# A hybrid of deformable convolution, additive attention and routed experts on one core: shorter square roots, queries through a mask, four banks for the first image's front, and the last image's end as ranked steps

## The chip, the cores and the metric

The kernel runs on one core of a Trainium2 chip, in single precision. The metric is the device time of one execution, in microseconds (us). The kernel before takes 15566.36 us, the median of three runs (15549.57 to 15602.39).

The names of the engines in what follows: PE is TensorE (matrix products; PEld are its weight loads), DVE is VectorE, ACT is ScalarE, POOL is GpSimd, SP is SyncE, which issues most of the DMAs. A suffix q, as in DVEq, is an engine's sequencer, which handles waits and drains.

## What is computed

Eight images of 56 x 56 pixels and 128 channels, so 3136 tokens an image, go through two layers:

```
# layer 0
xp = x @ w_in + b_in
h  = gelu(batchnorm(depthwise3x3(x) + dw_b))
offset, mask = h @ w_off + b_off, softmax(h @ w_msk + b_msk)      # 4 groups x 9 samples
y  = sum over 9 samples of mask * bilinear(pad(xp), place + offset)
x  = x + gamma1 * layer_norm(y @ w_out + b_out)
x  = x + gamma2 * layer_norm(gelu(x @ w_fc1 + b_fc1) @ w_fc2 + b_fc2)
# layer 1, on t = tokens of x
u = ln(t); f = u @ W1[:128]; g = u @ W1[128:]                     # 16 columns each
e[i,j] = exp(tanh(f_i + g_j + b1) @ w2 + b2)  for j < i, else 0
t = t + (e / sum_j e) @ u
z = ln(t); p = softmax(z @ gate_w, over tokens)                   # 64 experts
each expert takes its top 8 tokens, pools them by p, runs 128-512-128 with gelu,
and adds p * result to those 8 tokens of t
```

Every layer norm and the batch norm need a reciprocal square root of a variance plus an epsilon. The attention's f is called the query, its g the key.

## The kernel before

**Tiling.** An image has 7 bands of 8 rows (`image_in`, `project_in`, the nine taps of `conv`, `offsets`, `weights`), 27 tiles of patches, 49 sample tiles of 64 positions and 25 blocks of 128 tokens (the last has 64). A band of x is transposed on TensorE (L1643, four transposes into one PSUM bank) and copied out by VectorE (L1199), projected (L1657, copied at L1207), and a patch tile is four transposes again (L1643), a copy by VectorE (L1215) and a DMA to DRAM (L949). From there GpSimd gathers the four corners of each sample by indirect DMA (L1104), 18 of them for a sample tile; VectorE multiplies them by their weights (L1285, six instructions) and adds them up (L1288). A block then goes through the chain of steps `turn`, `mix`, `turn_mid`, `hidden`, `mlp_out`, `turn_norm`, `keys`, which alternate between TensorE and VectorE in one PSUM bank (`chain_ps`). Attention takes keys and queries in units of one tanh on ScalarE (L1584) over 128 partitions, which are 8 rows of tokens by the 16 hidden values; TensorE multiplies by w2 (L1746), ScalarE takes exp (L1594), and TensorE turns it (L1643) and adds up the values (L1775); `finish` on VectorE ends the block.

**The root.** `rsqrt` (L1154 to L1165) is a bit trick and three Newton steps on one column: a sum (`var`, L1156), a scaled sum (`newton`, L1157), the first guess from the bits of `var` (L1159), and three times an instruction with two per-partition pointer operands (L1162) and one with one (L1164), with a `settle` (a drain, L1123) between them. A block calls it four times; with the one of the batch norm there are 801 calls.

**The queries.** `keys` on TensorE is one product with w_key (L1728, 128 columns) and eight with `w_query` (L1731, 16 columns each), which holds w_q in the columns of one of eight rows and zeros in the others: each of the eight picks every eighth token, so that the sum over the eight in PSUM has row q's query in partitions 16q to 16q+15. VectorE copies the keys (L1330) and adds b1 to the queries (L1331).

**The side bank.** All steps of SIDE (bands, patches, conv, offsets, routing, experts, combine) share one PSUM bank, `side_ps`: TensorE waits for its last reader (`side_free`) before each.

**The order.** Each engine executes its steps in an order that a planner works out when the kernel is built: `due_times` gives each step a time by which it is wanted, `needs` what it waits for, `LASTS` how long it is supposed to last, and `simulate` runs a list scheduling over several images, from which a period of two images is cut. Image 0 has an order of its own, images 1 to 6 are a loop of three double periods, and image 7 has the last order, into which `late_steps` put the routing of images 0 to 6 (u_), their experts (w_in, e_) and the combine (c_in, c_x, c_mix L1855, c_store; 49 combine steps, each one TensorE step of 4 instructions). What image 7 itself still needs after its last block is written by hand behind that: SP L1064 to L1081, VectorE L1489 to L1545, ScalarE L1607 to L1615, TensorE L1858 to L1925. In this order it is: max (L1491), exp on ScalarE (L1609) beside match_replace (L1495) and not_equal (L1497), the product (L1502), turns and pooling (L1643, L1867), then 16 steps of four experts each (L1805, L1811), whose weights arrive in five slots of which 11 are loaded again (L1051, L1054), the last mix (L1921) and the saves (L1080).

## Time and profile before

| | us |
|---|---|
| median of three runs | 15566.36 |
| the profiled execution | 15422.14 |
| its span, first to last instruction | 15420.3 |
| TensorE busy (matmuls) | 8049.2 (52%) |
| ScalarE busy | 6799.7 (44%) |
| GpSimd busy | 6705.1 (43%) |
| VectorE busy | 6160.4 (40%) |
| mean granted TensorE clock | 0.694 of full |

The busy times are sums over all instructions of an engine, in one execution. No engine is busy for much more than half of the span, so the sums alone don't say what sets the time; for that the profile follows the chain of waits back from the last instruction, and its shares are of the span. Times of single instructions come from the timeline, whose origin is the first instruction.

### The profile page before, as it was taken

How to read it: one execution, taken by the hardware profiler on the slowest of the kernel's cores; microseconds unless marked ns; L12 is line 12 of the kernel's file. 1: busy time of each engine (PE TensorE's matmuls, PEld its weight loads, DVE VectorE, ACT ScalarE, POOL GpSimd, SP SyncE). 2: the span in 40 equal slices, each digit the busy share in tenths (PEclk: the TensorE clock that was granted, in tenths of full speed). 3: DMA queues.
4: the chain of work that ended last, by engine and by line, in shares of the span. 5: the costliest groups of instructions: out<-in, count | busy, mean ns of one | idle time of the engine just before them, and what ended most of it. 6: DMA issues, size and time to landing. Idle time of an engine off the chain costs nothing.

```text
span 15420.3 us, 158696 instructions
## 1 busy us (share of the span) xinstructions
PE 8049.2 (52%) x48713; PEld 4360.0 (28%) x48713; DVE 6160.4 (40%) x17991; ACT 6799.7 (44%) x8233; POOL 6705.1 (43%) x7060
## 2 busy tenths in 40 slices
PE   3445554555644556445554555544555455544568
PEld 1222222222322223222232222222222222222234
DVE  3443334433344334433344433443434433444342
ACT  0234553445534555245443455434543345533454
POOL 4444344444444444444444444444444444444420
PEclk7566776667766777667676676667766667766778
DMA  1111111111111111111111111111111111211234
GB/s 57 41 50 35 31 40 41 48 34 33 40 42 47 34 34 42 44 42 32 37 42 46 40 34 37 42 46 38 32 40 40 49 35 31 57 54 53 76 105 144
DMA packets 453515, 711.92 MB, mean 46 GB/s; under 512 B 146641, under 2 KB 260754, under 8 KB 451026
## 3 DMA queue, kind: packets, MB, share of 16 engines
q0 software_dynamic: 225792, 462.87, 11.4%
q1 hardware_dynamic: 226866, 238.69, 4.9%
q8 instruction: 407, 6.67, 0.2%
q14 instruction: 450, 3.69, 0.1%
HBM read 595.03 MB, written 105.96 MB: 45 GB/s over the span
## 4 chain that ended last, share of the span: by engine, by line
another core or an unknown queue 35%; PE 18%; DVE 15%; ACT 13%; issue 13%; DVEq 5%; DMA 1%; SPq 0%; POOL 0%; ACTq 0%; POOLq 0%
ACT tanh L1584 12%; PE score_ps L1746 6%; DVEq L1123 5%; DVE pool_mem L1285 3%; DVE newton L1162 2%; PE value_ps L1775 2%; PE chain_ps L1731 2%; DVE rstd L1164 2%; PE turn_ps L1643 1%; PE chain_ps L1711 1%; PE side_ps L1674 1%; DVE bst L1169 1%; PE side_ps L1643 1%; PE chain_ps L1719 1%
## 5 line engine op out<-in xcount | busy, mean ns | idle before, releaser
L1584 ACT ACTIVATE tanh<-key_rep,query 128x896 f32<-128x896 f32 (+7 forms) x6400 | 5563.3, 951 | 5580.4 <-remote 2489.4
L1104 POOL DMA_INDIRECT pool_mem<-patches_even,pool_mem x3528 | 3352.2, 950 | 4120.9 <-DVE y L1288 2961.6
L1104 POOL DMA_INDIRECT pool_mem<-patches_odd,pool_mem x3528 | 3352.7, 950 | 4102.6 <-DVE y L1288 3079.5
L1746 PE MATMUL score_ps<-tanh,score_w 128*32 128x512 f32 (+3 forms) x24320 | 3530.2, 634 | 2116.0 <-ACT tanh L1584 1289.8
L1746 PEld LDWEIGHTS score_ps<-tanh,score_w 128*32 128x32 f32 x24320 | 819.4, 124 | 4196.5 <-issue 2606.8
L1285 DVE TENSOR_TENSOR pool_mem<-pool_mem 128x384 f32<-128x384 f32 x2352 | 1136.1, 553 | 41.2 <-issue 37.8
L1775 PE MATMUL value_ps<-values,expoT 128*128 128x129 f32 (+1 forms) x5200 | 1002.7, 342 | 258.7 <-issue 185.3
L1288 DVE TENSOR_REDUCE y<-pool_mem 128x64 f32<-128x2304 f32 x392 | 1000.9, 2553 | 38.3 <-issue 8.9
L1775 PEld LDWEIGHTS value_ps<-values,expoT 128*128 128x128 f32 (+1 forms) x5200 | 882.3, 244 | 355.5 <-issue 289.5
L1643 PE MATMUL turn_ps<-ident,expo 128*128 128x128 f32 (+1 forms) x2632 | 590.4, 348 | 727.5 <-ACT expo L1594 320.8
L1594 ACT ACTIVATE expo<-score_ps,tiny 128x896 f32<-128x896 f32 (+9 forms) x416 | 383.4, 922 | 1054.3 <-remote 713.4
L1352 DVE COPY expoT<-turn_ps 128x512 f32<-128x512 f32 (+4 forms) x800 | 456.3, 571 | 857.2 <-remote 568.6
L1162 DVE TENSOR_SCALAR newton<-rstd,newton 128x1 f32<-128x1 f32 (+1 forms) x2403 | 655.1, 273 | 231.9 <-issue 50.0
L1643 PEld LDWEIGHTS turn_ps<-ident,expo 128*128 128x128 f32 (+1 forms) x2632 | 396.1, 181 | 923.2 <-issue 361.1
L1330 DVE COPY key_rep<-chain_ps 128x128 f32<-128x128 f32 (+1 forms) x200 | 57.6, 288 | 1490.1 <-remote 1178.0
L1731 PEld LDWEIGHTS chain_ps<-chainT,w_query 128*128 128x128 f32 x3200 | 635.8, 303 | 0.0
L1731 PE MATMUL chain_ps<-chainT,w_query 128*128 128x16 f32 (+1 forms) x3200 | 620.6, 342 | 0.0
L1164 DVE TENSOR_SCALAR rstd<-newton,rstd 128x1 f32<-128x1 f32 (+1 forms) x2403 | 513.4, 214 | 230.5 <-issue 51.1
L1728 PE MATMUL chain_ps<-chainT,w_key 128*128 128x128 f32 (+1 forms) x400 | 137.7, 443 | 782.9 <-DVE chainT L1323 655.9
L1169 DVE BATCH_NORM_STATS2 bst<-chain_ps 128x6 f32<-128x128 f32 (+1 forms) x400 | 118.5, 296 | 1062.2 <-remote 677.1
L1594 ACT ACT_TABLE_LOAD x207 | 265.6, 1283 | 617.9 <-remote 451.6
L1323 DVE COPY chainT<-chain_ps 128x128 f32<-128x128 f32 (+1 forms) x200 | 57.1, 286 | 1176.2 <-remote 1075.5
(167 smaller groups left out, 7470.3 us busy)
## 6 DMA issues: line engine op xcount, KB each, us to landing
pool_mem<-in_weight SPq DMA_DIRECT2D x64, 1024.0 KB, 10.1
pool_mem<-patches_even,pool_mem POOLq DMA_INDIRECT x3528
pool_mem<-patches_odd,pool_mem POOLq DMA_INDIRECT x3528
patches_even<-pool_mem SPq DMA_DIRECT2D x104, 256.0 KB
patches_odd<-pool_mem SPq DMA_DIRECT2D x104, 256.0 KB
pool_mem<-in_x SPq DMA_DIRECT2D x56, 224.0 KB
x_tok<-in_x SPq DMA_DIRECT2D x192, 64.0 KB
x_d<-x SPq DMA_DIRECT2D x192, 64.0 KB
```

The lines of the kernel that those rows point to most:

```text
L1104: pool.indirect_dma_start(gathered[:, b, j * 4 * CG:(j + 1) * 4 * CG], None, patches_flat[int(odd)], bass.IndirectOffsetOnAxis(ap=index[:, ...
L1123: return v.drain()
L1162: v.tensor_scalar(newton[:r, 1:2], rstd[:r], rstd[:r], newton[:r, 0:1], ALU.mult, ALU.mult)
L1164: v.tensor_scalar(rstd[:r], newton[:r, 1:2], 1.5, rstd[:r], ALU.add, ALU.mult)
L1285: v.tensor_tensor(part, part, weight[:, lo:lo + PIECE].unsqueeze(2) .to_broadcast([P, PIECE, CG, 4]), ALU.mult)
L1288: v.tensor_reduce(y[:, i // 2 % 2, b].rearrange("p (g c) -> p g c", c=CG), product.rearrange("p (g t) c k -> p g c t k", g=2), AX_XY, ALU. ...
L1584: nc.scalar.activation(tanh[:, ui % TANH_SLOTS, :w], key_rep[:, lo:lo + w], ACT.Tanh, bias=query[:, col:col + 1]).then_inc(tanh_done.sem, 1)
L1594: nc.scalar.activation(expo[:r, ci % 2, :w], score_ps[:r, ci % 2, :w], ACT.Exp, bias=tiny[:r, 2:3])\
L1643: return mm(out, src, ident[:r, :r], is_transpose=True, start=True, stop=True)
L1731: last = mm(chain_ps[:, P:P + r // ROWS8], w_query[:, q].rearrange("p a b -> p (a b)"), chainT[:, q:r:ROWS8], start=q == 0, stop=q == ROWS ...
L1746: last = mm(score_ps[32 * col:32 * col + 32, ci % 2, lo:hi], score_w[:, place], tanh[:, ui % TANH_SLOTS, lo:hi], start=place == 0, stop=pl ...
L1775: last = mm(value_ps[:r, :C + 1], expoT[:wj, pi % 2, z, :r], values[:wj, value_place(odd, j)], start=j == 0, stop=j == k)
```

## The change

- **Roots.** `var` goes: the first guess is taken from the bits of `newton`'s first column with another constant. The first instruction of a Newton step becomes a scalar_tensor_tensor, with one pointer operand and one tensor of one column, the second a scalar_tensor_tensor with a constant and one tensor.
- **Queries.** One product with a w_q that is laid out eight times (128 columns), instead of eight of 16 columns. VectorE adds b1 and multiplies the 128 x 128 result by a mask of zeros and ones (`own_row`, a new constant that comes by one more DMA), drains, and adds up groups of eight columns. The zeroing of `w_query` and its eight copies at the start go.
- **Image 0's front.** Its 7 bands and 27 patch tiles take turns in four banks (the quarters of `score_ps`) with a count of reads of their own, and the patches are copied to four buffers, with a semaphore each, in place of two.
- **Image 7's end.** The part written by hand becomes steps with rank 0 (`l_in` to `l_save`) of the last order, the combine of images 0 to 6 gets the lowest rank (due at 40), the expert weights have four slots in place of five (12 loads again), exp works in place and is started only when not_equal is done, and the experts' results and chosen rows lie on 128 partitions with two DMAs for the results and the second biases.
- **Costs.** The planner's costs of `keys`, `mix`, `mlp_out` and `finish` change with the first two parts, so that the order of every image is worked out anew.

```diff
-RSQRT_MAGIC = 1597463007.0
+RSQRT_MAGIC = 1597463007.0 - 2.0 ** 30 - 2.0 ** 22
...
-LATE_SLOTS = 5
-ROUTE_AT = (4.0, 7.0, 10.0, 14.0)
+LATE_SLOTS = 4
+SLOTS_AT = (19600, 15504, 11408, 7312)
+ROUTE_AT = (2.0, 5.0, 8.0, 11.0)
...
+EARLY_BANKS = 4
...
-    ("pe", "turn_norm"): .35, ("pe", "keys"): 2.3, ("pe", "route"): .35, ("pe", "logits"): .45,
+    ("pe", "turn_norm"): .35, ("pe", "keys"): .9, ("pe", "route"): .35, ("pe", "logits"): .45,
...
+    ("dve", "l_max"): 10.5, ("act", "l_exp"): 3.3, ("dve", "l_mul"): 3.8, ("pe", "l_turn"): .9, ("dve", "l_turn"): .5,
...
-            able = [x for x in ready[e] if side_free or e != "pe" or x[2][0] not in SIDE]
+            able = [x for x in ready[e] if e != "pe" or x[2][0] not in SIDE or
+                    (banks[began % EARLY_BANKS] if x[1:] in early else side_free)]
...
     done = sum(len(images) for images in units)
+    when = 40.0
     for n in range(done):
-        when += COMBINE_GAP
+        when += .1
...
-        put(when + s * .01, "sp", ("w2_in", s), at("dve", "sample", NSUB - 1),
-            *([at("sp", "c_store", done - 1, q) for q in range(turns)] if s >= 3 else []))
+        put(25.0 + s * .01, "sp", ("w2_in", s), at("dve", "sample", NSUB - 1),
+            *([at("sp", "e_store", STEPS - 1)] if s >= 3 else []))
...
+    put(0, "sp", ("l_in",), *last_block)
+    put(0, "dve", ("l_max",), at("sp", "l_in"), at("dve", "u_last", last))
+    put(0, "act", ("l_exp",), at("dve", "l_max"))
+    put(0, "dve", ("l_mul",), at("act", "l_exp"))
...
+    for s in range(STEPS):
+        if s >= LATE_SLOTS:
+            put(s * .01, "sp", ("l_w", s), at("sp", "w2_in", LATE_SLOTS - 1), at("pe", "l_out", s - LATE_SLOTS))
...
...
-            v.memset(w_query[:], 0.0)
...
-            for i in range(ROWS8):
-                v.tensor_copy(w_query[:, i, i], w_q[:])
-
...
-                v.tensor_scalar(var[:r], src, EPS, None, ALU.add)
                 v.tensor_scalar(newton[:r, 0:1], src, EPS, -0.5, ALU.add, ALU.mult)
                 settle()
-                v.tensor_scalar(rstd[:r].bitcast(I32), var[:r].bitcast(I32), -0.5, RSQRT_MAGIC, ALU.mult, ALU.add)
+                v.tensor_scalar(rstd[:r].bitcast(I32), newton[:r, 0:1].bitcast(I32), -0.5, RSQRT_MAGIC, ALU.mult, ALU.add)
                 settle()
                 for _ in range(3):
-                    v.tensor_scalar(newton[:r, 1:2], rstd[:r], rstd[:r], newton[:r, 0:1], ALU.mult, ALU.mult)
-                    settle()
-                    v.tensor_scalar(rstd[:r], newton[:r, 1:2], 1.5, rstd[:r], ALU.add, ALU.mult)
+                    v.scalar_tensor_tensor(newton[:r, 1:2], rstd[:r], rstd[:r], newton[:r, 0:1], ALU.mult, ALU.mult)
+                    settle()
+                    v.scalar_tensor_tensor(rstd[:r], newton[:r, 1:2], 1.5, rstd[:r], ALU.add, ALU.mult)
                     settle()
...
                     v.tensor_copy(key_rep[:, at:at + r], chain_ps[:, :r])
-                    v.tensor_scalar(query[:, i * A:i * A + r // ROWS8], chain_ps[:, P:P + r // ROWS8], tiny[:, 0:1],
-                                    None, ALU.add)
+                    v.scalar_tensor_tensor(spread[:, :r], chain_ps[:, P:P + r], tiny[:, 0:1], own_row[:, :r], ALU.add, ALU.mult)
+                    settle()
+                    v.tensor_reduce(query[:, i * A:i * A + r // ROWS8], spread[:, :r].rearrange("p (g q) -> p g q", q=ROWS8),
+                                    AX_X, ALU.add)
                     settle().then_inc(keys_copied.sem, 1)
...
+                elif what == "l_max":
+                    dve.wait_ge(last_in, 16)
+                    v.max(top[:E], score7)
+                    settle()
+                    v.tensor_scalar(neg[:E], top[:E, 0:1], -1.0, None, ALU.mult)
+                    v.match_replace(chosen7, top[:E], score7, LOW)
+                    settle()
+                    v.tensor_tensor(chosen7, score7, chosen7, ALU.not_equal)
+                    settle().then_inc(last_top, 1)
...
-            v.tensor_scalar(neg[:E], top[:E, 0:1], -1.0, None, ALU.mult)
-            settle().then_inc(last_top, 1)
-            v.match_replace(chosen7, top[:E], score7, LOW)
...
+                    nc.scalar.activation(score7, score7, ACT.Exp, bias=neg[:E], accum_out=total[:E, 0:1])
...
+            def bank_free(n, step):
+
+                if not is_early(n):
+                    side_free()
+                    return side_ps[:]
+                at = early_steps.index(step)
+                if at >= EARLY_BANKS:
+                    pe.wait_ge(early_read, early_reads.index(early_steps[at - EARLY_BANKS]) + 1)
+                return early_bank[at % EARLY_BANKS]
...
-                    for q in range(ROWS8):
-
-                        last = mm(chain_ps[:, P:P + r // ROWS8], w_query[:, q].rearrange("p a b -> p (a b)"),
-                                  chainT[:, q:r:ROWS8], start=q == 0, stop=q == ROWS8 - 1)
-                    last.then_inc(keys_done.sem, 1)
+                    mm(chain_ps[:, P:P + r], w_q[:].rearrange("p a b -> p (a b)"), chainT[:, :r], start=True, stop=True)\
+                        .then_inc(keys_done.sem, 1)
...
+        "own_row": (np.arange(P)[:, None] // A == np.arange(P)[None, :] % ROWS8).astype(np.float32),
```

**Places where the order changes.** The first is the start of TensorE's program, image 0's bands and patches; `side_ps` and `score_ps` are PSUM, `pool_mem` and `early` hold the x bands, the padded planes and the depthwise taps. Rows with `ident` are transposes, 128x448 once is a projection, and 128x448 x9 is the depthwise conv. Before:

```order
L1643 MATMUL side_ps<-ident,pool_mem 128x112 x8
L1657 MATMUL side_ps<-pool_mem,early 128x448
L1643 MATMUL side_ps<-ident,pool_mem 128x112 x8
L1657 MATMUL side_ps<-pool_mem,early 128x448
L1643 MATMUL side_ps<-ident,pool_mem 128x112 x12
L1657 MATMUL side_ps<-pool_mem,early 128x448 x5
L1643 MATMUL side_ps<-ident,pool_mem 128x128 x104
L1643 MATMUL side_ps<-ident,pool_mem 36x128 x4
L1674 MATMUL side_ps<-pool_mem,early 128x448 x9
```

After:

```order
L1746 MATMUL score_ps<-ident,pool_mem 128x112 x8
L1760 MATMUL score_ps<-pool_mem,early 128x448
L1746 MATMUL score_ps<-ident,pool_mem 128x112 x8
L1760 MATMUL score_ps<-pool_mem,early 128x448
L1746 MATMUL score_ps<-ident,pool_mem 128x112 x8
L1760 MATMUL score_ps<-pool_mem,early 128x448
L1746 MATMUL score_ps<-ident,pool_mem 128x112 x4
L1760 MATMUL score_ps<-pool_mem,early 128x448 x4
L1746 MATMUL score_ps<-ident,pool_mem 128x128 x52
L1777 MATMUL side_ps<-pool_mem,early 128x448 x9
L1746 MATMUL score_ps<-ident,pool_mem 128x128 x52
L1746 MATMUL score_ps<-ident,pool_mem 36x128 x4
```

All of these steps go through `score_ps` now, transposes run further ahead of projections, and the first band's conv stands in the middle of the patches.

The second is the first `keys` step on VectorE, in image 0, with its neighbours (`key_rep` takes the keys, `query` the queries, `spread` is the masked product). Before:

```order
L1248 SCALAR_TENSOR_TENSOR pool_mem<-pool_mem,base_index 128x126
L1330 COPY key_rep<-chain_ps 128x128
L1331 TENSOR_SCALAR query<-chain_ps,tiny 128x16
L1285 TENSOR_TENSOR pool_mem<-pool_mem 128x384 x6
L1288 TENSOR_REDUCE y<-pool_mem 128x64
```

After:

```order
L1335 SCALAR_TENSOR_TENSOR pool_mem<-pool_mem,base_index 128x126
L1417 COPY key_rep<-chain_ps 128x128
L1418 SCALAR_TENSOR_TENSOR spread<-chain_ps,tiny,own_row 128x128
L1420 TENSOR_REDUCE query<-spread 128x16
L1280 COPY pool_mem<-side_ps 128x8x56
L1381 COPY chainT<-chain_ps 128x128
```

Two instructions stand where one did, and another patch copy and chain copy follow in place of a sample tile's products: the steps around it have moved too.

The third is the end of TensorE's program, from the last block's gate logits (L1787 before, L1887 after) on: the transposes and products of 64 columns are image 7's turns and pooling, and the rows of 112x128 are the combine (L1855 before, L1958 after). Before:

```order
L1787 MATMUL side_ps<-xln2T,gate_w 64x64
L1643 MATMUL score_ps<-ident,tanh 112x64 x8
L1867 MATMUL value_ps<-key_rep,tanh 64x128 x4
L1643 MATMUL score_ps<-ident,tanh 112x64 x4
L1867 MATMUL value_ps<-key_rep,tanh 64x128 x4
L1643 MATMUL score_ps<-ident,tanh 112x64 x4
L1867 MATMUL value_ps<-key_rep,tanh 64x128 x4
```

After, the same place, and then the end of the expert loop:

```order
L1887 MATMUL side_ps<-xln2T,gate_w 64x64
L1958 MATMUL side_ps<-pool_mem 112x128 x16
L1746 MATMUL score_ps<-ident,tanh 112x64 x8
L1978 MATMUL value_ps<-key_rep,tanh 64x128 x8
L1746 MATMUL score_ps<-ident,tanh 112x64 x8
L1978 MATMUL value_ps<-key_rep,tanh 64x128 x8
L1746 MATMUL score_ps<-ident,tanh 112x64 x8
L1978 MATMUL value_ps<-key_rep,tanh 64x128 x8
L1746 MATMUL score_ps<-ident,tanh 112x64 x4
L1958 MATMUL side_ps<-pool_mem 112x128 x4
L1978 MATMUL value_ps<-key_rep,tanh 64x128 x4
L1958 MATMUL side_ps<-pool_mem 112x128 x4
```

```order
L1913 MATMUL score_ps<-pool_mem,expoT 1x128 x16
L1746 MATMUL chain_ps<-ident,expo 128x128 x4
L1958 MATMUL side_ps<-pool_mem 112x128 x4
L1913 MATMUL score_ps<-pool_mem,expoT 1x128 x16
L1958 MATMUL side_ps<-pool_mem 112x128 x8
L2012 MATMUL score_ps<-x_tok,tanh 112x128 x28
L1958 MATMUL side_ps<-pool_mem 112x128 x4
```

Before, no combine step stands behind the last gate logits; now 13 of the 49 do: four ahead of the first turn, three among turns and pooling, two in the expert loop, and four around the last mix (L2012). Four more stand just ahead of the last logits, among the last block's turns of exp.

## Rows read from the trace of the kernel before

**Rows 1.** The page's busy times by engine.

```profile
PE 8049.2 (52%) x48713; PEld 4360.0 (28%) x48713; DVE 6160.4 (40%) x17991; ACT 6799.7 (44%) x8233; POOL 6705.1 (43%) x7060
```

**Rows 2.** The chain of waits, whole span: shares by line.

```profile
by line: another core or an unknown queue 35.3%; issue 12.7%; ACT tanh L1584 11.6%; PE score_ps L1746 6.3%; DVEq L1123 5.1%; DVE pool_mem L1285 2.7%; DVE newton L1162 2.5%; PE value_ps L1775 2.1%; PE chain_ps L1731 2.0%; DVE rstd L1164 1.9%
```

**Rows 3.** The page's groups: line, op, out<-in xcount | busy, mean ns | idle before.

```profile
L1104 POOL DMA_INDIRECT pool_mem<-patches_even,pool_mem x3528 | 3352.2, 950 | 4120.9 <-DVE y L1288 2961.6
...
L1162 DVE TENSOR_SCALAR newton<-rstd,newton 128x1 f32<-128x1 f32 (+1 forms) x2403 | 655.1, 273 | 231.9 <-issue 50.0
...
L1330 DVE COPY key_rep<-chain_ps 128x128 f32<-128x128 f32 (+1 forms) x200 | 57.6, 288 | 1490.1 <-remote 1178.0
...
L1731 PE MATMUL chain_ps<-chainT,w_query 128*128 128x16 f32 (+1 forms) x3200 | 620.6, 342 | 0.0
L1164 DVE TENSOR_SCALAR rstd<-newton,rstd 128x1 f32<-128x1 f32 (+1 forms) x2403 | 513.4, 214 | 230.5 <-issue 51.1
L1728 PE MATMUL chain_ps<-chainT,w_key 128*128 128x128 f32 (+1 forms) x400 | 137.7, 443 | 782.9 <-DVE chainT L1323 655.9
```

**Rows 4.** VectorE groups by form, same columns as rows 3.

```profile
L1187 DVE SCALAR_TENSOR_TENSOR ln_a<-chain_ps,mv,affine 128x128 f32<-128x128 f32 x384 | 134.8, 351 | 30.1 <-issue 1.3
...
L1331 DVE TENSOR_SCALAR query<-chain_ps,tiny 128x16 f32<-128x16 f32 x192 | 43.2, 225 | 0.0
...
L1228 DVE TENSOR_REDUCE pool_mem<-pool_mem 128x14 f32<-128x126 f32 x56 | 15.9, 284 | 6.6
...
L1178 DVE SCALAR_TENSOR_TENSOR early<-early,chan 128x1 f32<-128x1 f32 x1 | 0.2, 220 | 0.1
...
L1176 DVE TENSOR_TENSOR early<-rstd,chan 128x1 f32<-128x1 f32 x1 | 0.2, 160 | 0.1
```

**Rows 5.** Timeline of VectorE, one root: start us, us, engine, line, op.

```profile
5037.77 0.15 DVE L1156 TENSOR_SCALAR var<-mv 128x1 f32<-128x1 f32 x1
5037.84 0.14 DVE L1157 TENSOR_SCALAR newton<-mv 128x1 f32<-128x1 f32 x1
...
5038.30 0.27 DVE L1162 TENSOR_SCALAR newton<-rstd,newton 128x1 f32<-128x1 f32 x1
5038.65 0.21 DVE L1164 TENSOR_SCALAR rstd<-newton,rstd 128x1 f32<-128x1 f32 x1
5038.94 0.27 DVE L1162 TENSOR_SCALAR newton<-rstd,newton 128x1 f32<-128x1 f32 x1
```

**Rows 6.** Timeline of one keys step on TensorE.

```profile
4997.01 3.43 PE L1731 MATMUL chain_ps<-chainT,w_query 128*128 128x16 f32 x16
```

**Rows 7.** Timeline of all engines after that step.

```profile
5026.76 0.95 POOL L1104 DMA_INDIRECT pool_mem<-patches_even,pool_mem  x1 [0.30 <-issue]
5032.91 0.29 DVE L1330 COPY key_rep<-chain_ps 128x128 f32<-128x128 f32 x1 [32.45 <-remote]
```

**Rows 8.** Windows: stretch, its length, busy us of engines, clock, DMA share, GB/s.

```profile
0.00:51.60 51.60, 19.90 (x42) 8.16 (x43) 22.41 (x55) 0.00 (x0) 0.20 (x4) 1.00 0.24 66
51.60:104.70 53.10, 30.02 (x108) 19.05 (x108) 17.99 (x26) 0.00 (x0) 0.00 (x0) 1.00 0.33 127
...
15043.50:15260.00 216.50, 211.59 (x1298) 129.28 (x1300) 61.93 (x144) 173.24 (x177) 0.00 (x0) 0.91 0.42 122
```

**Rows 9.** Window of the last expert loop's transfers.

```profile
15324.00:15386.00 62.00, 40.86 (x524) 21.10 (x528) 13.63 (x35) 2.59 (x12) 0.00 (x0) 0.78 1.04 372
```

**Rows 10.** Timeline of image 0's patches.

```profile
55.49 1.12 PE L1643 MATMUL side_ps<-ident,pool_mem 128*128 128x128 f32 x4 [0.83 <-DVEq L1123]
56.65 0.69 DVE L1215 COPY pool_mem<-side_ps 128x512 f32<-128x512 f32 x1 [1.25 <-PE side_ps L1643]
```

**Rows 11.** Timeline of GpSimd: the first gather.

```profile
124.10 1.08 POOL L1104 DMA_INDIRECT pool_mem<-patches_even,pool_mem  x1 [123.64 <-DVEq L1123]
```

**Rows 12.** Groups by line: the combine on TensorE.

```profile
L1855 PE MATMUL side_ps<-pool_mem 64*112 64x128 f32 x392 | 93.0, 384 | 1.7 <-issue 1.0 <-DVEq L1123 0.7
```

**Rows 13.** Timeline of ScalarE: image 7's softmax.

```profile
15290.65 2.91 ACT L1609 ACTIVATE pool_mem<-tanh,early 64x3136 f32<-64x3136 f32 x1 [23.26 <-DVEq L1123]
```

More of the change, by code:

```diff
@@ L410, in simulate @@
     for n, engine, step in todo:
-        before = {(n - age, e, s) for age, e, s in need[engine, step]} & known
+        before = {(n - age, e, s) for age, e, s in need.get((n, engine, step), need[engine, step])} & known
         waiting[n, engine, step] = len(before)
@@ L725, in network @@
         bias1 = late.take(E * (HID // P)).rearrange("p (e c) -> p e c", e=E)
-        bias2 = late.take(C)[:E]
+        bias2 = late.take(C)
         acc = late.take(C)
```

419 lines of the change are left out of this document (243 added, 176 removed).

## The prediction

> **What bounds the kernel now.** I read the busy times first. TensorE is busy for 52% of the span, ScalarE 44%, GpSimd 43%, VectorE 40% [rows 1]: no engine sets the time alone, so a saving counts only where its engine is what the others wait for. The chain of waits says where: 35.3% of the span is waiting that no instruction explains, 11.6% the tanh, 6.3% its product with w2, 5.1% VectorE's drains; of what the change touches, L1162 has 2.5%, L1164 1.9% and the queries' product L1731 2.0% [rows 2]. The unexplained part has a pattern. At 4997.01 TensorE does the queries of a block and is done at 5000.44 [rows 6]; VectorE's copy that waits for them starts at 5032.91, 32.45 us idle, and the last gather of a burst started at 5026.76 [rows 7]. A gather takes 0.95 us and 0.30 until the next, so the 18 of a sample tile are a burst of 22.5 us, and 392 tiles are 8820 us, 57% of the span [rows 3, 7]. A hand-over from TensorE inside a burst can thus come late by more than any edit here saves, and what is gained ahead of it is then given back. Over the 200 blocks that copy idles 1490.1 us, 1178.0 of it released by nothing visible [rows 3].
>
> All sums are made against the profiled execution, 15422.14 us; the median of the runs is 15566.36, 0.93% above it, and I carry a difference in us over to the median unchanged.
>
> **Roots.** Of the first two instructions, which start 0.07 us apart, one goes [rows 5]: 0.07 us. The instruction with two pointer operands takes 273 ns, with one 214 [rows 3]. On one column, a scalar_tensor_tensor with one pointer and a tensor takes 220 ns, and a tensor_tensor without a pointer 160 [rows 4]. So each of three pairs becomes 380 from 487 ns, 0.107 less, and the gaps between them (the pair's starts are 0.35 and 0.29 apart, 0.08 above the durations [rows 5]) stay: 0.07 + 3 x 0.107 = 0.39 us a root, 801 roots, 312 us of VectorE. Its two lines hold 4.4% of the chain, 679 us, of 1168.5 busy [rows 2, 3]: 58% of them lie on the path. 0.58 x 312 = 181 us. The bounds are nothing (the forms cost the same as now) and 312.
>
> The Trainium skill, "ScalarE: Activation LUTs", section "What ACT_TABLE_LOAD costs", says that on ScalarE each per-partition pointer operand adds about 93 ns. The rows above show about 60 on VectorE, so the measured number goes into the sum; by 93 the roots would give about a half more.
>
> **Queries, TensorE.** 16 passes of 16 columns take 3.43 us at the lower clock of that stretch [rows 6]; over the span L1731 is busy 620.6 us for 200 blocks. The new product has the form of L1728, busy 137.7 for 200 [rows 3]. That is 483 us less. L1731's share of the chain is 2.0%, 308 us, half of its busy time [rows 2, 3], so 240 us on the path; bounds 0 and 483.
>
> **Queries, VectorE.** The addition of 16 columns, 225 ns, gives way to 128 columns from PSUM with a pointer and a tensor, 351 (L1187), a drain of about 0.1 (the gaps above), and a reduction as L1228's 126 columns, 284 [rows 4]: 0.51 us more, 102 us over 200 blocks. Every tanh of the block waits behind it, and so does the next block's `turn`, which needs chain_ps free; I take 60% as on the path, 60 us, bounds 40 and 102. The eight copies and the zeroing at the start are about 2 to 4 us, against one more constant to load: nothing.
>
> Steady part: -181 - 240 + 60 = -361 us if the chain's shares are taken at their word. But 57% of the time is burst, and there a step that is done earlier may only wait longer for the same hand-over. I count the part outside (43%) whole and the part inside by half: 0.715 x 361 = 258 us.
>
> **The new order of all images.** The planner's costs for four steps change and with them every period. No row prices that. The nearest is the unexplained wait itself, 35.3% or 5443 us: a tenth more or less of it would be 540 either way. I take 0, and keep it for the range.
>
> **Image 0's front.** The bands end at 51.60 and the patches at 104.70 [rows 8]: 53.1 us for 27 patches, 1.97 each. In one of them TensorE works 1.12 us and is idle 0.83 before it, for VectorE's copy of 0.69 and the drain behind it [rows 10]: the two take turns because there is one bank. With four, TensorE, the slower, goes on: 27 x 0.83 = 22 us less. The 7 bands are 14 steps with the same kind of copy between them: 14 x 0.83 = 12 us less. And the first conv stands between patches now, so that its gelu and offsets run beside them; before, 19.4 us lay between the end of the patches and the first gather at 124.10 [rows 8, 11]. Of that I take 6. Together 40 us. The share of the DMA queues there is 0.33 at 1.97 a tile [rows 8]; at 1.14 it would be 0.57, so they hold. If each patch still waits for its store, half is left: bounds 20 and 48. What follows waits for nothing else, so this is carried to the end.
>
> **Image 7's end.** From 15043.50 to 15260 TensorE is busy 211.59 of 216.50 us [rows 8]: there it is the bound, and the combine is on it. The combine's 49 steps are x392, busy 93.0, so 1.90 us each [rows 12]. In the new order 13 stand behind the last gate logits and 4 just ahead of them: 17 x 1.90 = 32 us out of that stretch. What takes them in: four lie in front of the first turn while VectorE works (free), two in the expert loop, which waits for DMA (free), three among turns and pooling and four around the last mix: 7 x 1.9 = 13 us, of which I take 10; the four among the last turns half, 4. Then exp of 2.91 us, which ran beside match_replace, comes behind not_equal: +3 [rows 13]. And the DMA queues, full for 62.0 us (share 1.04) with 11 loads [rows 9], get a twelfth: +5.6. -32 + 10 + 4 + 3 + 6 = -9; with what is freed earlier in the stretch by the shorter roots nothing, since TensorE bounds it. Bounds -35 and +20.
>
> **Sum.** -258 - 40 - 9 = -307: 15115 for a profiled execution, 15566 - 307 = 15,260 for the median.
>
> **Rivals.**
>
> A, the bursts swallow it: hand-overs inside bursts end with the burst whatever comes before, and of the part outside only half meets no other wait. 361 x 0.43 x 0.5 = 78, with 49 of the ends 127: 15,440. For it: the 32 us of [rows 7] against a saving of 3. Against it: the chain passes through L1162, L1164 and L1731 for 987 us, so they are often what is waited for.
>
> B, everything counts: VectorE and TensorE are in order, and whatever shortens the chain of one block lets the next sample tile's products, and so the next burst, start earlier. 312 + 483 - 102 = 693, with 49: 742, so 14,825. For it: GpSimd idles 4120.9 us on one parity's gathers, mostly for VectorE's products [rows 3].
>
> C, slower: the new order puts more hand-overs from TensorE behind bursts. Its place is the periods of images 1 to 6, its price the length of such a wait, up to 32 us [rows 7]. It decides from 307 us more, 5.6% of the 5443, or one such wait for every 20 blocks of the 200 (10 x 32). With 8% it is +435 - 307 = +128: 15,695. For it: no cost of the planner stands for a late hand-over, so its places are chance. Against it: the order before was made by the same rule, so the chance is even on both sides, and needs 5.6% to win.
>
> D, VectorE's new forms hold up the gathers. Each root has six instructions with two tensors from SBUF where it had none: 6 x 0.19 x 801 = 913 us, 57% of it in bursts, 520 us. A gather that falls on one (520 / 1.25 = 416 of them) would start later by half of its length, 0.1 us: 40 us, so 15,300; 10% of the weight. If each instruction held up a whole burst by its full length it were +520, and slower by 213.
> That a VectorE instruction with two SBUF inputs takes a port pair that GpSimd needs, and blocks it for its whole length, is in the Trainium skill, "SBUF — State Buffer", in the list on the diagram of the ports; rows 7 show gathers 1.25 us apart, but none beside such an instruction, so they don't settle it.
>
> **How the numbers follow.** The forecast has 0.46, A 0.22, B 0.10, C 0.12, D 0.10 (nearly all of it faster). About 0.3%, 47 us, is what a measurement of this kernel can tell from no change. Within it lies the upper end of A with an unlucky order: 0.07. Slower is C with 0.12 and 0.01 of D: 0.13. Faster is the rest, 0.80. The range starts between the forecast and B, 14,970, and ends at 15,560, which leaves most of C and half of B outside.
>
> **What would show it.** Roots: each VectorE pair 380 ns with gaps of 0.08, a root 2.06 us; wrong if the forms take 273 and 214 as before. Queries: two passes and busy about 140 us in place of 620; the wait of the keys' copy tells A (unchanged at about 7.5 us a block) from B. Front: the first gather near 84 in place of 124. End: 17 combine steps after the last keys' stretch, the expert loop's full queues some 68 us long. The order: the share of unexplained wait, 35.3%, up in C. Gathers further apart than 1.25 us would be D. The prediction is wrong if what lies between the first gather and the last stretch (124.10 to 15043.50 [rows 8, 11]) shortens by less than 80 or more than 600 us.

## The result, and the profile after

The changed kernel takes 15361.55 us, the median of four runs (15339.42 to 15399.26), against 15557.97 of the kernel before in its four: a ratio of 0.9879, 95% interval 0.9853 to 0.9904, 196 us less. The forecast was 307 us less. The sign and the order of size came out, but two of its large terms did not, and it will be seen that their errors took each other away in large part.

The two profiled executions stand oddly to this: 15422.14 us before, 136 below its median, and 15399.26 after, 38 above its own. Compared to each other they would give 23 us. So only the two ends are compared from trace to trace, and the middle is what is left of the difference of the medians. In the traces of related kernels below the start repeats within 3 us (121.92 to 124.10 with the old front, 72.12 and 74.45 with the new), the end less well.

The changed kernel's busy times from the page, and two of its groups (columns as in [rows 3]):

```profile
PE 7675.1 (50%) x45913; PEld 3859.4 (25%) x45913; DVE 5935.6 (39%) x17381; ACT 6773.1 (44%) x8210; POOL 6700.8 (44%) x7060
...
L1243 DVE SCALAR_TENSOR_TENSOR newton<-rstd,newton 128x1 f32<-128x1 f32 (+1 forms) x2403 | 528.3, 220 | 211.4 <-issue 34.9
...
L1245 DVE SCALAR_TENSOR_TENSOR rstd<-newton,rstd 128x1 f32<-128x1 f32 (+1 forms) x2403 | 385.7, 161 | 222.0 <-issue 31.8
```

Against [rows 1], TensorE has 374 us less and VectorE 225 less. The root's instructions take 220 and 161 ns where they took 273 and 214 [rows 3]. The timeline of one root on VectorE:

```profile
5012.25 0.15 DVE L1238 TENSOR_SCALAR newton<-mv 128x1 f32<-128x1 f32 x1
...
5012.71 0.22 DVE L1243 SCALAR_TENSOR_TENSOR newton<-rstd,newton 128x1 f32<-128x1 f32 x1
5013.01 0.16 DVE L1245 SCALAR_TENSOR_TENSOR rstd<-newton,rstd 128x1 f32<-128x1 f32 x1
5013.24 0.22 DVE L1243 SCALAR_TENSOR_TENSOR newton<-rstd,newton 128x1 f32<-128x1 f32 x1
```

A pair starts 0.53 us after the last (5012.71 to 5013.24), where it was 0.64 [rows 5]; the whole root, to the end of its last instruction at 5014.24, is 1.99 us. The groups of the `keys` step (TensorE, then VectorE):

```profile
L1832 PE MATMUL chain_ps<-chainT,w_q 128*128 128x128 f32 (+1 forms) x400 | 117.6, 393 | 2.8 <-issue 2.8
...
L1418 DVE SCALAR_TENSOR_TENSOR spread<-chain_ps,tiny,own_row 128x128 f32<-128x128 f32 (+1 forms) x200 | 67.9, 340 | 0.0
...
L1417 DVE COPY key_rep<-chain_ps 128x128 f32<-128x128 f32 (+1 forms) x200 | 57.5, 288 | 650.8 <-remote 525.5 <-issue 62.7 <-PE chain_ps L1832 58.9
...
L1420 DVE TENSOR_REDUCE query<-spread 128x16 f32<-128x128 f32 (+1 forms) x200 | 56.7, 283 | 15.7 <-issue 0.8
```

The queries' product is busy 117.6 us where it was 620.6, and the copy of the keys waits 650.8 us in all where it waited 1490.1 [rows 3]. The chain of waits, by line:

```profile
by line: another core or an unknown queue 35.8%; issue 14.4%; ACT tanh L1677 13.4%; PE score_ps L1846 6.9%; DVEq L1208 4.8%; DVE pool_mem L1372 2.4%; PE value_ps L1875 1.9%; DVE newton L1243 1.7%; PE side_ps L1777 1.3%; DVE rstd L1245 1.3%;
```

L1731 had 2.0% of it [rows 2] and its heir is not among the ten; the roots have 1.7 and 1.3% for 2.5 and 1.9%; the unexplained part is 35.8% for 35.3%.

The front, in a window (columns as in [rows 8]), then rows of the timeline, then the first gather. The rows are the copy of the last band, four transposes of a patch tile, the convs, copies of patches, and the copy of the last patch tile:

```profile
0.00:72.00 72.00, 43.01 (x200) 26.63 (x201) 41.34 (x80) 4.62 (x5) 0.20 (x4) 0.96 0.46 148
```

```profile
37.53 0.69 DVE L1288 TENSOR_SCALAR pool_mem<-score_ps,chan 128x448 f32<-128x448 f32 x1 [0.21 <-PE score_ps L1760]
...
44.92 0.66 PE L1746 MATMUL score_ps<-ident,pool_mem 128*128 128x128 f32 x4 [1.74 <-DVEq L1208]
...
48.52 7.53 PE L1777 MATMUL side_ps<-pool_mem,early 128*128 128x448 f32 x18
48.61 0.69 DVE L1302 COPY pool_mem<-score_ps 128x512 f32<-128x512 f32 x1 [0.20 <-issue]
...
49.51 0.69 DVE L1302 COPY pool_mem<-score_ps 128x512 f32<-128x512 f32 x1 [0.20 <-issue]
...
56.53 0.69 DVE L1302 COPY pool_mem<-score_ps 128x512 f32<-128x512 f32 x1 [5.43 <-PE score_ps L1746]
...
68.18 0.68 DVE L1302 COPY pool_mem<-score_ps 36x512 f32<-36x512 f32 x1 [0.20 <-issue]
```

```profile
74.45 1.08 POOL L1189 DMA_INDIRECT pool_mem<-patches_even,pool_mem  x1 [73.99 <-DVEq L1208]
```

Where it is not held up, VectorE copies a patch every 0.90 us (48.61, 49.51), of which it works 0.69: there it sets the pace, not TensorE. The convs that now stand among the patches hold it up for 5.43 us (56.53). The first gather starts at 74.45 in place of 124.10 [rows 11], 49.7 us earlier. For the parts of this, the same two copies before:

```profile
50.81 0.68 DVE L1207 TENSOR_SCALAR pool_mem<-side_ps,chan 128x448 f32<-128x448 f32 x1 [2.00 <-PE side_ps L1657]
...
104.71 0.68 DVE L1215 COPY pool_mem<-side_ps 36x512 f32<-36x512 f32 x1 [1.24 <-PE side_ps L1643]
```

The bands end at 38.22 in place of 51.49, 13.3 us earlier; the patches last 30.6 us (to 68.86) in place of 53.9 (to 105.39), 23.3 less; and from there to the first gather it is 5.6 in place of 18.7, 13.1 less.

The last two gathers, and image 7's softmax (rows of the timeline):

```profile
14965.78 0.96 POOL L1189 DMA_INDIRECT pool_mem<-patches_odd,pool_mem  x1 [0.30 <-issue]
14967.04 0.95 POOL L1189 DMA_INDIRECT pool_mem<-patches_odd,pool_mem  x1 [0.30 <-issue]
```

```profile
15256.51 3.42 DVE L1577 TENSOR_TENSOR tanh<-tanh 64x3136 f32<-64x3136 f32 x1
15259.99 2.91 ACT L1700 ACTIVATE tanh<-tanh,early 64x3136 f32<-64x3136 f32 x1 [39.09 <-DVEq L1208]
...
15263.00 0.69 DVE L1568 TENSOR_TENSOR pool_mem<-pool_mem,side_ps 112x512 f32<-112x512 f32 x1 [2.20 <-PE side_ps L1958]
...
15264.06 3.48 DVE L1583 SCALAR_TENSOR_TENSOR tanh<-tanh,early 64x3136 f32<-64x3136 f32 x1
```

From the last gather at 14967.04 to the end of the span, 15397.4, there are 430.4 us; before it was 492.4 (14927.94 to 15420.3). The exp starts at 15259.99, when not_equal is done, and a combine step (L1568) fills VectorE meanwhile. The window of the expert loop's transfers:

```profile
15300.00:15372.00 72.00, 48.36 (x551) 25.99 (x552) 15.78 (x40) 2.80 (x13) 0.00 (x0) 0.74 0.94 335
```

The DMA engines are full to 0.94 for 72 us, where it was 1.04 for 62.0 with one load fewer [rows 9].

Of the 196 us, then, the front has 50 and what follows the last gather 62; the 14.8 milliseconds between have only 84, where 258 were forecast. By the two traces alone that middle is 89 us longer than before (14892.6 for 14803.8), so the 84 rests on the medians and on ends that are taken as the same in every execution.

### The profile page after: what moved, and what is told of

Same layout as the page of the kernel before. It is cut to its first block, busy times and chain, and to the rows that moved or that the text cites. A ratio compares the mean times of both kernels' runs of the same rounds, so it can differ in the third digit from the quotient of the medians.

```text
span 15397.4 us, 152662 instructions
## 1 busy us (share of the span) xinstructions
PE 7675.1 (50%) x45913; PEld 3859.4 (25%) x45913; DVE 5935.6 (39%) x17381; ACT 6773.1 (44%) x8210; POOL 6700.8 (44%) x7060
## 4 chain that ended last, share of the span: by engine, by line
another core or an unknown queue 36%; ACT 16%; PE 16%; issue 14%; DVE 12%; DVEq 5%; DMA 1%; SPq 0%; POOL 0%; ACTq 0%; POOLq 0%
ACT tanh L1677 13%; PE score_ps L1846 7%; DVEq L1208 5%; DVE pool_mem L1372 2%; PE value_ps L1875 2%; DVE newton L1243 2%; PE side_ps L1777 1%; DVE rstd L1245 1%; PE turn_ps L1746 1%; PE chain_ps L1814 1%; ACT expo L1687 1%; DVE bst L1250 1%; ACT L1687 1%; PE chain_ps L1822 1%
## 5 line engine op out<-in xcount | busy, mean ns | idle before, releaser
L1846 PE MATMUL score_ps<-tanh,score_w 128*32 128x512 f32 (+3 forms) x24320 | 3703.9, 650 | 2566.8 <-ACT tanh L1677 1562.2
L1846 PEld LDWEIGHTS score_ps<-tanh,score_w 128*32 128x32 f32 x24320 | 855.6, 126 | 4803.6 <-issue 2891.3
L1375 DVE TENSOR_REDUCE y<-pool_mem 128x64 f32<-128x2304 f32 x392 | 1000.9, 2553 | 36.0 <-issue 6.7
L1243 DVE SCALAR_TENSOR_TENSOR newton<-rstd,newton 128x1 f32<-128x1 f32 (+1 forms) x2403 | 528.3, 220 | 211.4 <-issue 34.9
L1814 PE MATMUL chain_ps<-chainT,w_fc 128*128 128x128 f32 (+1 forms) x1600 | 338.6, 379 | 501.1 <-DVE chainT L1394 418.8
L1777 PE MATMUL side_ps<-pool_mem,early 128*128 128x448 f32 x1008 | 427.5, 581 | 108.1 <-DVEq L1208 107.0
L1245 DVE SCALAR_TENSOR_TENSOR rstd<-newton,rstd 128x1 f32<-128x1 f32 (+1 forms) x2403 | 385.7, 161 | 222.0 <-issue 31.8
L1814 PEld LDWEIGHTS chain_ps<-chainT,w_fc 128*128 128x128 f32 x1600 | 300.8, 280 | 599.2 <-DVE chainT L1394 459.9
```

Source lines behind the costliest of these rows:

```text
L1243: v.scalar_tensor_tensor(newton[:r, 1:2], rstd[:r], rstd[:r], newton[:r, 0:1], ALU.mult, ALU.mult)
L1375: v.tensor_reduce(y[:, i // 2 % 2, b].rearrange("p (g c) -> p g c", c=CG), product.rearrange("p (g t) c k -> p g c t k", g=2), AX_XY, ALU. ...
L1777: last = mm(side_ps[:, :BAND], taps[:, t], x_pad[:, i * BAND_ROWS + dy:(i + 1) * BAND_ROWS + dy, dx:dx + W], start=t == 0, stop=t == TAPS - 1)
L1814: last = mm(chain_ps[:, c * P:c * P + r], w_fc1[:, c * P:(c + 1) * P], chainT[:, :r], start=True, stop=True)
L1846: last = mm(score_ps[32 * col:32 * col + 32, ci % 2, lo:hi], score_w[:, place], tanh[:, ui % TANH_SLOTS, lo:hi], start=place == 0, stop=pl ...
```

## The experiments

"This" and "before" were run on the same chip within one batch; between batches the level moves (the kernel before has medians of 15558, 15600 and 15420 us), so ratios are compared. The us given for single changes follow from the ratios; the medians alone would differ from them by up to 17 us. Where the gathers lie in each profiled execution (their first and last start, from the timeline of GpSimd, and the span):

| kernel | ratio | 95% | first gather | last gather | end after it |
|---|---|---|---|---|---|
| before | 1 | | 124.10 | 14927.94 | 492.4 |
| changed | 0.9879 | 0.9853 to 0.9904 | 74.45 | 14967.04 | 430.4 |
| roots alone | 0.9948 | 0.9934 to 0.9962 | 121.92 | 15034.21 | 489.5 |
| queries alone | 0.9763 | 0.9750 to 0.9776 | 123.89 | 14755.08 | 482.4 |
| costs alone | 1.0101 | 1.0086 to 1.0116 | 123.17 | 15283.46 | 454.7 |
| roots, queries, costs | 0.9905 | 0.9889 to 0.9920 | 122.92 | 14977.46 | 439.0 |
| roots, queries | 0.9737 | 0.9723 to 0.9750 | 122.91 | 14536.83 | 483.5 |
| changed, old costs | 0.9730 | 0.9717 to 0.9743 | 72.12 | 14526.17 | 476.2 |

**Roots alone** (e1_roots), with `var` taken out and the same two scalar_tensor_tensors, in the old order:

```diff
-                    v.tensor_scalar(newton[:r, 1:2], rstd[:r], rstd[:r], newton[:r, 0:1], ALU.mult, ALU.mult)
+                    v.scalar_tensor_tensor(newton[:r, 1:2], rstd[:r], rstd[:r], newton[:r, 0:1], ALU.mult, ALU.mult)
```

> The kernel before with the new roots alone, order untouched. Theory W (savings in front of a late hand-over from TensorE are given back, whatever the order): about a third of 181 us, so -60 us against before (ratio 0.996). Rival O (the two edits bring what was forecast and the new order takes it back): 0.715 x 181, so -130 us (ratio 0.992). VectorE busy 310 us less under both.

Measured: 15525.56 for 15599.66, 0.52% or 81 us less. VectorE's busy time fell by 304 us (6160.4 to 5856.0), of which about a quarter shows. The size is nearer to theory W here, 0.996 being within the interval and theory O's 0.992 outside.

**Queries alone** (e2_queries): the one product, the mask, the reduction, `own_row`, and none of the `w_query`.

```diff
-                    for q in range(ROWS8):
...
-                    last.then_inc(keys_done.sem, 1)
+                    mm(chain_ps[:, P:P + r], w_q[:].rearrange("p a b -> p (a b)"), chainT[:, :r], start=True, stop=True)\
+                        .then_inc(keys_done.sem, 1)
...
```

> The kernel before with the queries through the mask alone, order untouched. Theory W: about a third of 240 - 60, so -60 us (ratio 0.996). Rival O: 0.715 x 180, so -130 us (ratio 0.992). TensorE busy 480 us less under both.

Measured: 15235.77, 2.37% or 370 us less, six times what theory W and three times what theory O gave it, and more than the whole change brings. The group of the keys' copy:

```profile
L1327 DVE COPY key_rep<-chain_ps 128x128 f32<-128x128 f32 (+1 forms) x200 | 57.1, 286 | 427.3 <-remote 313.4 <-issue 57.7 <-PE chain_ps L1728 53.9
```

It waits 427.3 us for 1490.1 before [rows 3], and the part that nothing visible ends falls from 1178.0 to 313.4, in 36 such waits for 70 before. But the late hand-overs have not gone with it. Added up over all groups, the waits that nothing visible ends are 5620 us on VectorE for 5695 before, and 4947 on ScalarE for 4122; and their share of the chain is 37.7% for 35.3%, some 300 us more. They meet other steps now. So it isn't shown which waits on the path the 370 us were, beyond the 308 us that L1731 itself had on the chain.

**New costs alone** (e3_costs): the kernel before, and in the planner's table (the changed entries, gathered from its lines)

```diff
-("pe", "keys"): 2.3, ("dve", "mix"): 4.0, ("dve", "mlp_out"): 7.6, ("dve", "keys"): .6, ("dve", "finish"): 4.4
+("pe", "keys"): .9, ("dve", "mix"): 3.5, ("dve", "mlp_out"): 6.7, ("dve", "keys"): 1.1, ("dve", "finish"): 3.9
```

> The kernel before with the planner's new costs of keys, mix, mlp_out and finish alone: the instructions are the same, only their order is new. Theory W: within 40 us of before. Rival O: +170 us (ratio 1.011).

Measured: 15740.04, 1.01% or 158 us more (140 by the medians), with only the order other than before. Theory W falls. It also ends 38 us sooner after the last gather, so the middle is the worse for it by more than the total shows.

**The three together** (e4_steady), with the old front and end:

> The kernel before with roots, queries and new costs together, with the old front and the old end. Both theories: about -85 us (ratio 0.9945), since the whole change measured -196 and its trace shows the first gather 50 us and the end 62 us earlier. If it is -200 us, the ends bring nothing in a median execution and the two traces mislead.

Measured: 0.9905. That is 148 us less, where 85 were expected from the traces' ends. The reason is in the table: most of the shorter end is there without the new end, 439.0 us for 492.4. The whole change (0.9879) is 40 us below this kernel, which front and end bring together, but give or take some 45.

**Roots and queries in the old order** (e5_old_order), so e4_steady with the costs of before:

> The kernel before with roots and queries together, in the old order (the four planner's costs as before). Theory O2 (what is lost is lost by the new order, about +2%): the two edits add up, 0.9948 x 0.9763 = 0.971 of before, 15150 us where before is 15600. Rival W2 (the edits overlap: what the queries gave back is the same wait that the roots shorten): not below the queries alone, 0.976.

Measured: 0.9737, 406 us less. It is 0.25% above what the two alone make together (0.9948 x 0.9763 = 0.9712) and 0.26% below the queries alone, just beyond the noise on either side, so the roots add about half of their small share. Against e4_steady it shows the price of the new order with these steps: 0.9905 - 0.9737, 1.7%, 260 us. The rows of tanh and of one parity's gathers, and what GpSimd waits for in all (us in total, times, longest), in e5_old_order, then in e4_steady:

```profile
L1581 ACT ACTIVATE tanh<-key_rep,query 128x896 f32<-128x896 f32 (+7 forms) x6400 | 5565.2, 951 | 4858.4 <-remote 2745.3
L1104 POOL DMA_INDIRECT pool_mem<-patches_even,pool_mem x3528 | 3345.9, 948 | 3923.1 <-DVE y L1283 2774.5
...
POOL pool_mem L1104 <- DVE y L1283: 5673.8, 342, 37.8
```

```profile
L1581 ACT ACTIVATE tanh<-key_rep,query 128x896 f32<-128x896 f32 (+7 forms) x6400 | 5558.5, 950 | 5750.5 <-remote 3155.5
L1104 POOL DMA_INDIRECT pool_mem<-patches_even,pool_mem x3528 | 3342.4, 947 | 4178.9 <-DVE y L1283 3031.5
...
POOL pool_mem L1104 <- DVE y L1283: 6118.7, 352, 42.2
```

These busy times are equal. In the new order GpSimd waits 445 us more for VectorE to be done with a sample tile (y, L1283), and that is where the middle, 440 us longer between the first and the last gather (14854.5 for 14413.9), has its length. It says where, not why. On the chain of the two kernels "issue" has 358 us more (12.6 to 14.6%), the product with w2 316 more (5.8 to 7.7%), tanh 233 less and the unexplained part 118 less; the matmuls, the same ones, are busy for 148 us more. Why these steps meet each other worse in the new order is open.

**The changed kernel with the old costs** (e6_after_old_costs): only the costs of e3_costs turned back.

> The changed kernel whole, with the planner's four old costs, so that the middle has nearly the old order, but the new front and the new end stay. Theory O2: 0.971 less 48 us of the front and 9 of the end, 0.9675, about 15090 us where before is 15600, faster than both kernels. Rival W2: the changed kernel's 0.988 within 0.3%.

Measured: 15001.68 for 15419.73, 0.9730, 418 us less, the fastest of all with every gather on this chip: 1.5% below the changed kernel. Both expectations missed, theory O2's 0.9675 by 85 us and rival W2's 0.988 by more. Against e5_old_order the new front and end bring only 0.07% (11 us, give or take 30) of the 58 that the two traces show at the ends (50.8 and 7.3); the stretch between first and last gather is 40 us longer. The changed kernel has 38 us more in that stretch than e4_steady, too, so most of what the front gains seems to be given back before the last gather. Why, is open.

**One gather of eighteen** (g1_before_one_gather, g2_after_one_gather): in both kernels

```diff
-                    for j in range(SAMPLES):
+                    for j in range(1):
```

and the wait for them to match. The kernels leave out 17 of 18 gathers, so what they sample is not right.

> The kernel before, of whose 18 gathers for a sample tile only the first is issued (the other 17 are left out, their buffer is zeroed once), all the rest as it is. If TensorE's late hand-overs come from the gathers, nearly none is later than 1 us and the time falls to 0.75 to 0.85 of before, though GpSimd was busy for 43% only. If they come from something else (instruction fetch, the clock), they stay and only GpSimd's own share on the path goes: 0.93 or more.

> The changed kernel with the same 17 of 18 gathers left out. Theory O2 (the new order is worse because of where the gathers lie): without gathers the new order costs nothing, and the changed kernel gains on the one before what its steps were priced at, 181 + 240 - 60 + 57, about 420 us or more. Rival (the new order is worse by itself): no more than 250 us.

Measured: 0.6011, well below the 0.75 to 0.85 expected, and 0.5886. With 17 of 18 gathers forty per cent of the time is gone; all of them had kept their engine busy for 43% of it. In g1_before_one_gather, the page's busy times and chain, and the keys' copy:

```profile
PE 6785.2 (73%) x48713; PEld 3797.3 (41%) x48713; DVE 6143.1 (66%) x17992; ACT 6772.5 (73%) x8233; POOL 370.6 (4%) x396
...
ACT 35%; PE 27%; DVE 18%; issue 11%; DVEq 7%; DMA 1%; SPq 0%; ACTq 0%
```

```profile
L1331 DVE COPY key_rep<-chain_ps 128x128 f32<-128x128 f32 (+1 forms) x200 | 57.3, 287 | 390.3 <-PE chain_ps L1732 368.0 <-ACT tanh L1585 21.6 <-issue 0.4
```

"Another core or an unknown queue", 35% of the chain before, is not there any more, and all but 0.4 us of the keys' copy's waits end with something visible. So on this chip the late hand-overs come with the gathers. In the trace of before they also lie there: of the 9817 us that VectorE and ScalarE wait for nothing visible, 8022 fall within bursts of gathers (less than 1.5 us apart), which are 57% of the span, and 6824 belong to waits that end within 5 us after a burst's last gather.

The changed kernel's gain is the same, though: 9271.57 - 9078.37 = 193 us without them, 196 with them. Theory O2 asked for 420 or more, so it falls, and its rival (no more than 250) stands: the whole gain is no smaller for the bursts. TensorE's granted clock, as a mean over the span, is 0.839 in g1_before_one_gather for 0.694 before, and its same matmuls are busy for 6785.2 us in place of 8049.2; a part of the 6148 us is therefore TensorE's own speed, and how much isn't separated.

The last four kernels ran on another chip, and there **the kernel before takes 9523.03 us**, not 15400 to 15600. Their ratios are to that.

**One gather, old costs** (g3_old_costs_one_gather):

> The changed kernel with the four old costs, and 17 of 18 gathers left out. Theory O3 (the new order is worse by itself, since it was 85 us less than forecast in the middle with and without gathers): as much below the changed kernel without gathers (0.5886 of before) as with them (0.973 against 0.988, 1.5% of the time): 0.580, 8940 us where before is 15420. Rival O2 (it is worse because of the gathers): 0.5886 within 0.15%.

Measured: 8862.33, ratio 0.9309. In us it is 216 below g2_after_one_gather, and 409 below g1_before_one_gather, as e6_after_old_costs is 418 below before with all gathers. It speaks for the new order being worse by itself, but it ran on another chip than the two, so it isn't shown.

**Plain DMAs** (g4_direct): the changed kernel with old costs, and

```diff
-                        pool.indirect_dma_start(
...
+                        pool.dma_start(gathered[:, b, j * 4 * CG:(j + 1) * 4 * CG],
+                                       patches_flat[int(odd)][j * P:(j + 1) * P]).then_inc(gather_done[b], 16)
```

> The changed kernel with the four old costs, where each of the 7056 gathers is a plain DMA of the same 128 rows of 512 bytes from GpSimd's queue (fixed rows, so what is sampled is left out). If TensorE's completions are held up by any DMA that GpSimd issues, or by the traffic: the time stays near 0.97 and a quarter of the completions is late. If it is the indirect form alone: no late completions, a time of 0.8 or less.

Measured: 8871.00, ratio 0.9316, as without gathers. On this chip no wait is unexplained even with indirect gathers (the next two kernels), so what it was to tell apart it doesn't. Its group shows 535 ns in place of the 967 of an indirect one on this chip:

```profile
L1189 POOL DMA_DIRECT2D pool_mem<-patches_odd x3528 | 1856.5, 535 | 2368.7 <-DVE y L1373 2305.4
```

**Old costs of keys only** (e7_root_costs_only, the changed kernel otherwise) and **old ranks in image 7** (e8_old_ranks), the second with

```diff
-ROUTE_AT = (2.0, 5.0, 8.0, 11.0)
+ROUTE_AT = (4.0, 7.0, 10.0, 14.0)
...
-    when = 40.0
...
```

and the gap of 1.0 between combines again, the last weights due behind them, and all four old costs.

> The changed kernel with the old costs of keys on both engines, but the new ones of mix, mlp_out and finish. If the cost of keys does the harm (TensorE's fell by 1.4, the largest share of a step): 0.973 as with all four old. If the three of the roots do: 0.988 as the changed kernel. If any change of the order is a draw of its own: a third value between or outside.

> The changed kernel with the four old costs, and with the old due times of routing, combine and last weights in image 7 (the steps l_ stay ranked). By the forecast's pricing of the end the combine out of TensorE's full stretch is worth 32 us and costs 23 elsewhere: 5 to 15 us slower than with the new ranks (0.9735). If the new ranks bring nothing or cost the last image's 20 us: 0.973 or 0.972.

Measured: 9437.96 (ratio 0.9909, 0.9892 to 0.9925) and 9471.82 (0.9944, 0.9928 to 0.9961). Neither answers its question, since both are bound by their gathers on this chip, as the rows show. In e7_root_costs_only, busy times and chain, then gathers and keys' copy:

```profile
PE 6436.9 (68%) x45913; PEld 3387.0 (36%) x45913; DVE 5925.0 (63%) x17381; ACT 6766.2 (72%) x8230; POOL 6827.7 (72%) x7060
...
POOL 61%; issue 21%; ACT 7%; PE 4%; DVE 4%; DMA 2%; DVEq 1%; SPq 0%; POOLq 0%; ACTq 0%
```

```profile
L1189 POOL DMA_INDIRECT pool_mem<-patches_odd,pool_mem x3528 | 3412.8, 967 | 1074.9 <-issue 1069.4 <-DVE y L1375 5.5
...
L1417 DVE COPY key_rep<-chain_ps 128x128 f32<-128x128 f32 (+1 forms) x200 | 57.1, 286 | 145.3 <-PE chain_ps L1832 128.4 <-ACT tanh L1677 14.6 <-issue 2.1
```

GpSimd has 61% of the chain, and its gathers follow each other at once: 1074.9 us idle for 3528 gathers, 0.30 each, no longer for VectorE. From the first gather to the last there are 8976.1 us in e7_root_costs_only (71.86 to 9047.94) and 8969.5 in e8_old_ranks (74.08 to 9043.55), though their orders differ: 7056 x 1.27. So between these two only what lies outside differs: e7 ends 393.3 us after the last gather and e8 432.6, 39 us of difference where the two spans differ by 35. In e8_old_ranks the first gather comes 50 us earlier than in the kernel before on the first chip, which would be its 51 us; the kernel before has no trace on this chip, so that it is bound in the same way there isn't shown.

## Why the prediction was right, and where it was not

That the total came as near the forecast as 196 to 307 is in good part luck: the queries brought 241 us more than their term, the new order cost 260 that stood in it as nothing.

**Roots.** 380 ns a pair and 0.39 us a root were right (0.107 a pair, as [rows 5] against the timeline after). The share on the path, 58%, was not: 81 us of 312 came out, 26%, for the 129 that stood in the sum.

**Queries.** The busy times were right: 503 us less on TensorE (620.6 to 117.6) for 483, and 340 + 283 ns on VectorE in place of 225. The price on the path was not: 129 us stood in the sum after all reductions, 370 came out. I had counted only the chain's 2.0% for L1731, and not that the keys' copy waited for this very product for 1490.1 us, 1178.0 of them released by nothing visible [rows 3]. Of these 865 went. The row was among mine; I used it as an argument against the gain. That it is the cause of the larger gain isn't shown, since at least as much of such waiting turned up at other steps (e2_queries).

**Half for what lies inside bursts** (the factor 0.715). No run bears it out: the whole gain is 196 us with the gathers and 193 without 17 of 18, and roots and queries together gave 406 us where the unreduced sum had 361. Rival A falls by the sign that was set for it, the keys' copy, whose wait went from 7.5 us a block to 3.3. Its thought, that late hand-overs end with the burst, fits the trace of before (e2_queries and g1_before_one_gather above); what it drew from it for the total does not.

**The new order, counted at nothing.** This is the term that failed: it costs 1.01% alone and 1.7% under the new steps, some 260 us. Rival C had it right in kind, place and even size (it decides at 307). Whether it had the cause is open. On the chain the unexplained share did not rise (33.5% in e3_costs for 35.3), but the waits for nothing visible of VectorE and ScalarE added up did, from 9817 to 10372 us. So what was forecast as -129 - 129 + 0 measured -81 - 325 + 260 (406 for the first two together), -146, and the ends make it the 196. The 260 is a difference of two of these runs, so that this sum closes proves nothing by itself.

**The middle.** The prediction was to be wrong if the middle shortened by less than 80 us. It is 84 by the medians, 4 above that mark and less than the noise, and by the two traces it is 89 longer (both from first to last gather). By its own sign it was at the edge.

**Front.** 50 us for 40 at the first gather. The bands (13.3 for 12) and the patches (23.3 for 22) came out, the patches with other parts than forecast: TensorE's four transposes take 0.66 us and not 1.12 (why, isn't shown), VectorE's pace is 0.90 a patch, and the convs among them cost 5.43. The term that was too small is what follows the patches, 13.1 for 6. But "carried to the end" was wrong as far as e6_after_old_costs against e5_old_order shows: of 58 us 11 arrive, give or take 30.

**End.** 9 us were forecast for the steps moved, and e6 against e5 has 7.3, the changed kernel against e4 8.6 (tails of 430.4 and 439.0). No run tells the five terms of that sum apart, so the agreement may be chance; the full queues last 10 us longer, not 6. Of the other 53 of the 62, some 9 came with roots and queries (492.4 to 483.5 in e5_old_order) and some 44 with the new costs (483.5 to 439.0), which stood in no term.

**D**, gathers held up by the new two-tensor forms: within a burst they still follow each other in 1.255 us on average, before as after, and take 950 ns; what GpSimd idles before gathers without waiting for anything visible is 2058.7 us before and 2053.8 after. The Trainium skill's rule on the shared port ("SBUF — State Buffer", section "SBUF: two separate sides", the list on the ports) has no visible price in this kernel. The Trainium skill states it there only against GpSimd instructions that read SBUF, a limit that the prediction left out.

## What to carry to other kernels

A planner's table of costs is part of the kernel: measure a new table alone, with no instruction changed, before it is shipped along with the edits that suggested it. Here edits worth 2.6% were shipped with an order that took 1.5 to 1.7% back, though the cost of `keys` on TensorE, for one, was truer than the old one (0.9 us for 2.3, its two products being busy for 1.3 a block). When a step's consumer waits for "nothing visible", the chain's share of the step bounds its price badly: shortening a step that had 308 us of the chain, and adding to its reader, gained 370. And a wait that goes at one step may turn up at the next, so add such waits up over all steps. And a profile tells of one chip: on another the same program takes 0.62 of the time, and two kernels near the changed one are bound by their gathers there.

## What the hardware showed that I had not expected

- On one chip, hand-overs from TensorE come late while GpSimd issues indirect gathers: of 15.4 ms, 6.1 are gone when 17 of 18 gathers are (9271.57 against 15419.73), though the gathers themselves are neither longer nor further apart (950 ns, 1.25 us) than on a chip where the kernel before takes 9523.03 us in all (967 ns, 1.27 us in e7_root_costs_only). Tanh (951 ns) and VectorE's large reduction (2553 ns) last the same on both. Whether TensorE ends late or its signal comes late, what differs between the chips, and whether plain DMAs would do it too, is open: g4_direct was to tell the last, and ran where nothing is late.
- The mean granted TensorE clock goes with it: 0.694 for the kernel before on that chip, 0.839 there with 17 of 18 gathers left out, 0.827 on the other chip with all of them. Which of the two follows from the other isn't shown.
- On VectorE a `[128,1]` instruction was 53 ns shorter with a one-column tensor in place of a pointer operand, in both places (273 to 220, 214 to 161).
- A plain DMA of 128 rows of 512 bytes occupies GpSimd for 535 ns, the indirect one for 967 on the same chip.
